# A fused GroupNorm and multi-scale linear attention kernel: TensorE's loop started at another point, its waits thinned, and two groups of small products mixed

## What is computed

```
xn  = group_norm(x, 32 groups)
qkv = einsum('nchw,oc->nohw', windows(xn, 4x4), qkv_w)
msq = concat([qkv, avg_pool5(qkv)], axis=1)          # full and pooled heads
q, k, v = relu(msq[..., :8]), relu(msq[..., 8:16]), msq[..., 16:]
v   = pad(v, one more column of ones)
kv  = einsum('ngld,nglm->ngdm', k, v)
out = einsum('ngld,ngdm->nglm', q, kv)
out = out[..., :-1] / (out[..., -1:] + 1e-15)
y   = einsum('nchw,oc->nohw', out, proj_w) * inv + offset
result = x + y
```

## Time and profile of the kernel before

| | |
|---|---|
| median of 3 runs | 928.52 us (928.47 to 930.1) |
| the profiled execution, its own time | 930.24 us |
| its span, first to last instruction | 928.3 us |
| around the span | 1.9 us |
| mean granted TensorE clock | 0.993 of full |
| TensorE matmul busy | 873.8 us, 94% |
| VectorE busy | 772.3 us, 83% |
| ScalarE busy | 609.5 us, 66% |
| GpSimd busy | 456.0 us, 49% |

### The profile page before, as it was taken

One profiled execution on the slowest core, in us unless ns is written; L12 is line 12 of the kernel. 1 busy time (PEld: TensorE's weight loads), 2 busy tenths in 40 slices (PEclk: granted clock), 3 DMA queues, 4 the chain that ended last, 5 costly groups with the idle time before them and its releaser, 6 DMA issues.

```text
span 928.3 us, 65376 instructions
## 1 busy us (share of the span) xinstructions
PE 873.8 (94%) x29282; PEld 733.4 (79%) x29282; DVE 772.3 (83%) x1625; ACT 609.5 (66%) x1542; POOL 456.0 (49%) x967
## 2 busy tenths in 40 slices
PE   0689999999999999999999999999999999999997
PEld 0578888888888888888888888888888888888885
DVE  7369989998878898998878998999887878787886
ACT  0457676767676767676766667676767676767673
POOL 1545454545454545555554545454545454545550
PEclk9999999999999999999999999999999999999998
DMA  9910000000000000000000000000000000000000
GB/s 378 431 50 17 26 17 26 17 26 17 25 19 25 26 17 26 17 26 17 26 17 26 18 26 17 26 17 27 17 26 17 25 25 18 26 17 26 18 26 27
DMA packets 15893, 38.77 MB, mean 42 GB/s; under 512 B 1888, under 2 KB 14688, under 8 KB 15456
## 3 DMA queue, kind: packets, MB, share of 16 engines
q1 hardware_dynamic: 15840, 38.26, 10.6%
HBM read 19.38 MB, written 18.87 MB: 41 GB/s over the span
## 4 chain that ended last, share of the span: by engine, by line
PE 93%; issue 3%; DVE 2%; POOL 1%; DMA 0%; ACT 0%; DVEq 0%; POOLq 0%
PE ps L611 23%; PE ps L582 19%; PE ps L538 14%; PE ps L549 9%; PE ps L556 9%; PE ps L633 7%; PE ps L627 6%; PE ps L635 4%; PE ps L558 4%; DVE stats L377 1%; DMA x_all<-x 0%; POOL hs L234 0%; DVE kvc_full L446 0%; POOL xp L234 0%; ACT o_sb L325 0%
## 5 line engine op out<-in xcount | busy, mean ns | idle before, releaser
L255 POOL TENSOR_TENSOR xn<-x_all,mean_t 128x384 f32<-128x384 f32 x96 | 79.4, 827 | 393.6 <-PE ps L558 375.1
L305 ACT ACTIVATE vm_pool<-ps,cst 128x256 f32<-128x256 f32 x576 | 225.5, 543 | 0.4 <-PE ps L549 0.4
L446 DVE TENSOR_TENSOR kvc_full<-ps,cst 128x864 f32<-128x864 f32 x192 | 193.7, 1050 | 17.8 <-PE ps L582 17.6
L446 DVE TENSOR_TENSOR kvc_pool<-ps,cst 128x864 f32<-128x864 f32 x192 | 193.2, 1048 | 0.0
L305 ACT ACTIVATE vm_full<-ps,cst 128x384 f32<-128x384 f32 x384 | 192.2, 598 | 0.9 <-PE ps L538 0.9
L312 ACT ACTIVATE q_full<-ps 128x384 f32<-128x384 f32 x96 | 47.2, 491 | 208.5 <-PE ps L556 208.5
L538 PE MATMUL ps<-wkv_sb,xn 128*128 128x128 f32 x1152 | 145.5, 276 | 23.5 <-POOL xn L256 23.5
L538 PEld LDWEIGHTS ps<-wkv_sb,xn 128*128 128x128 f32 x1152 | 144.1, 193 | 23.5 <-issue 23.5
L452 DVE SCALAR_TENSOR_TENSOR x_all<-ps,shift,x_all 128x384 f32<-128x384 f32 x96 | 59.3, 618 | 93.4 <-PE ps L633 93.2
L611 PEld LDWEIGHTS ps<-kvc_full,q_full 64*32 64x32 f32 x9216 | 99.5, 105 | 26.4 <-issue 26.3
L611 PE MATMUL ps<-kvc_pool,q_pool 64*32 64x72 f32 x9216 | 115.8, 230 | 2.1 <-issue 2.1
(11 more groups left out here) (66 smaller groups left out, 1242.2 us busy)
## 6 DMA issues: line engine op xcount, KB each, us to landing
out<-x_all SPq DMA_DIRECT2D x96, 192.0 KB, 1.9
x_all<-x SPq DMA_DIRECT2D x3, 4608.0 KB, 32.1
x_all<-x SPq DMA_DIRECT2D x6, 768.0 KB, 8.1
cst<-consts SPq DMA_DIRECT2D x1, 172.0 KB, 11.0
wkv_sb<-wkv SPq DMA_DIRECT2D x1, 128.0 KB, 10.8
o_sb<-proj SPq DMA_DIRECT2D x1, 128.0 KB, 10.4
wq_sb<-wq SPq DMA_DIRECT2D x1, 64.0 KB, 10.5
bn_sb<-bn SPq DMA_DIRECT2D x1, 2.0 KB, 10.3
```

Source lines behind the costliest of these rows:

```text
L255: link(pool.tensor_tensor(xr, src, mean, ALU.subtract), 1)
L305: last = act.activation(heads[:, :, e, :, 0:D], src, ACT.Copy, scale=col(mask + e))
L446: last = dve.tensor_tensor(kvc[:, g], src.to_broadcast(shape), own, ALU.mult)
```

## The change

TensorE's step is cut at another place of the same cycle. It now begins with transposes(s-1), and ends with Q(s+1) and the full K and V of s+2. The full kv products of strip s+1 no longer follow the pooled out products of strip s: the two are mixed in `out_pooled_and_kv`, two window groups of out products (32 instructions) and then one tile of kv products (16 instructions), three times. The waits of both stand ahead of the mixed block, among them the one for `y_done`. Waits that another wait implies are left out. `y_done` is no longer raised by the memset, and who waits for it waits for one less. Two steps at the start and two at the end now stand outside the loop, which has 46 rounds in place of 47. The other engines' streams are unchanged, but for the memset and SyncE's count.

```diff
-                    sp.wait_ge(y_done, t + (b * SPB + 2))
+                    sp.wait_ge(y_done, t + (b * SPB + 1))
...
-            dve.memset(dev[:], 0.0).then_inc(y_done, 1)
...
             def conv_kv_pooled(s, p):
                 pe.wait_ge(xp_ready, s + 1)
-                wait(pe, qm_f, s)
                 wait(pe, qm_p, s)
...
             def conv_q(s, p):
-                pe.wait_ge(km_p, s + 1)
                 pe.matmul(ps[:, Q_F, 0:SP], wq_sb[:], xn[:, p], start=True, stop=True).then_inc(q_f, 1)
-                pe.wait_ge(vm_p, s + 1)
                 pe.matmul(ps[:, Q_P, 0:SPP], wq_sb[:],
...
+            def kv_tile(pooled, t):
+                k, vm, bank, n = (k_pool, vm_pool, KVP, EP * KC) if pooled else (k_full, vm_full, KVF, EF * KC)
+                for r in range(G):
+                    rows = slice(H64 * r, H64 * (r + 1))
+                    for i in range(4):
+                        last = pe.matmul(ps[Q4 * i:Q4 * (i + 1), bank + r, t * n:(t + 1) * n],
+                                         k[rows, t, Q4 * i:Q4 * (i + 1)], vm[rows, t, :, i, :],
+                                         start=True, stop=True)
+                return last
...
+            def kv_products(s):
+                wait(pe, y_done, s - 1)
+                pe.wait_ge(vm_f, s + 1)
+                pe.nop(nofuse=True)
...
+            def kv_products_pooled(s):
+                pe.wait_ge(vm_p, s + 1)
+                wait(pe, num_f, s)
+                pe.nop(nofuse=True)
...
+            def out_products(s):
+                if is_last(s):
+                    pe.wait_ge(qm_p, s + 1)
+                pe.wait_ge(kvc_p, s + 1)
+                pe.nop(nofuse=True)
...
+            def out_pooled_and_kv(s):
+                pe.wait_ge(vm_f, s + 2)
+                wait(pe, y_done, s)
+                pe.nop(nofuse=True)
+                groups = [(t, e) for t in range(TP) for e in range(WP)]
+                for i in range(TF):
+                    for t, e in groups[QG * i:QG * (i + 1)]:
+                        last = out_tile(True, t, e)
+                    if i == TF - 1:
+                        last.then_inc(out_p, 1)
+                    last = kv_tile(False, i)
+                last.then_inc(kv_f, 1)
...
             def transposes(s):
-                pe.wait_ge(num_f, s + 1)
-                pe.wait_ge(num_p, s + 1)
                 if not is_last(s):
                     pe.wait_ge(kvc_f, s + 2)
                 else:
-                    pe.wait_ge(y_done, s + 1)
+                    pe.wait_ge(num_p, s + 1)
+                    pe.wait_ge(y_done, s)
...
             def step(s, p):
-                kv_products(s, False)
-                kv_products(s, True)
-                conv_q(s, p)
-                if not is_last(s):
-                    conv_kv(s + 1, 1 - p)
                 if not is_first(s):
                     transposes(s - 1)
                 if not is_last(s):
                     conv_kv_pooled(s + 1, 1 - p)
                 if not is_first(s):
                     project(s - 1)
-                out_products(s, False)
-                out_products(s, True)
+                out_products(s)
+                if is_last(s):
+                    out_products_pooled(s)
+                else:
+                    out_pooled_and_kv(s)
+                    kv_products_pooled(s + 1)
+                    conv_q(s + 1, 1 - p)
+                if not is_last(s) and not is_last(s + 1):
+                    conv_kv(s + 2, p)
...
+            kv_products(0)
+            kv_products_pooled(0)
+            conv_q(0, 0)
+            conv_kv(1, 1)
             step(0, 0)
-            with pe.Fori(1, NS - 1, 2) as s:
-                step(s, 1)
-                step(s + 1, 0)
-            step(NS - 1, (NS - 1) % 2)
+            step(1, 1)
+            with pe.Fori(2, NS - 2, 2) as s:
+                step(s, 0)
+                step(s + 1, 1)
+            step(NS - 2, 0)
+            step(NS - 1, 1)
```

More of the change, by code:

```diff
@@ L603, in out_products, with out_tile @@
+            def out_tile(pooled, t, e):
+                q, kvc, bank, wins = (q_pool, kvc_pool, OUTP, WP) if pooled else (q_full, kvc_full, OUTF, WF)
                 n = QG * KC
                 blocks = q[:].rearrange("p n e j -> p n (e j)")
[L605 to L613, removed]
@@ L614, in out_products @@
-                last.then_inc(done, 1)
+                for g in range(G):
+                    rows = slice(H64 * g, H64 * (g + 1))
+                    for c in range(4):
+                        r, w = c // QG, t * QG * wins + c % QG * wins + e
+                        last = pe.matmul(ps[Q4 * c:Q4 * (c + 1), bank + g, t * n:(t + 1) * n],
+                                         blocks[rows, 4 * t + c, Q4 * e:Q4 * (e + 1)], kvc[rows, r, w],
+                                         start=e == 0, stop=e == wins - 1)
@@ new lines, in out_tile @@
+                return last
+            def kv_products(s):
+                wait(pe, y_done, s - 1)
+                pe.wait_ge(vm_f, s + 1)
+                pe.nop(nofuse=True)
+                for t in range(TF):
+                    last = kv_tile(False, t)
+                last.then_inc(kv_f, 1)
[3 more added lines that the diff above has]
+                pe.nop(nofuse=True)
+                for t in range(TP):
+                    last = kv_tile(True, t)
+                last.then_inc(kv_p, 1)
@@ new lines, in out_products, with out_products_pooled @@
+            def out_products(s):
[3 more added lines that the diff above has]
+                pe.nop(nofuse=True)
+                for t in range(TF):
+                    for e in range(WF):
+                        last = out_tile(False, t, e)
+                last.then_inc(out_f, 1)
+            def out_products_pooled(s):
+                for t in range(TP):
+                    for e in range(WP):
+                        last = out_tile(True, t, e)
+                last.then_inc(out_p, 1)
```

## The result

The changed kernel takes **934.10 us** (median of 6 runs, 933.69 to 936.54), against 930.36 us for the kernel before (6 runs, 928.47 to 931.02): a ratio of 1.005, with a 95% interval of 1.0034 to 1.0066. It is slower, by 3.7 us, where 3 us of gain were forecast. The first three of the six runs of the kernel before are the ones behind the 928.52 us above. The profiled execution took 934.4 us, with a span of 932.6; it is set against the 930.24 and 928.3 of the one before.

What follows compares the result with a forecast made beforehand. TensorE with an exposed branch and a ring through ScalarE were taken to alternate as bound. Steady strips -5.1 us and cold code +2.1 gave -3.0: 925.5 us against the median, range 919.5 to 936.

Steps and rivals of the forecast that it cites:

- What bounds the kernel now: Steps alternate: 9.31 us, TensorE with the branch exposed, and 9.06 us, bound through ScalarE; shortening TensorE pays down to 9.06.
- The ring through ScalarE: Pooled kv, Q, ScalarE's relu_q and copies, then pooled kv again: 9.06 us a step, left as is by the change.
- the branch: The loop's compare-and-branch, 0.45 us in every second step; moved before the transposes, 0 left on the array, other bound 0.45.
- The dropped waits: Waits left out of TensorE's stream: 0.12 us gained between pooled out and full kv, nothing from the others, which are hidden.
- the ring through VectorE: Later out_p delays VectorE's pooled divide, then own_heads, statistics and residual: 9.08 us a step with bn_stats, 8.06 without.
- The mixed block: Mixed pooled out and full kv products: 1.72 us to the next pooled kv, nearly the plain sum of 1.74.
- D: Time from the mixed block's first matmul to the next pooled kv: 1.72 us taken, 1.52 to 2.28 possible.
- the slower rival: Changing between the two kinds of small matmul is not free; at D = 1.90 it gives 935.6 us; chance 0.25.
- The new wait and what is late next: The block waits for y_done, 0.2 us of new stall, hidden under 9.06; VectorE's pooled divide then waits for pooled out.
- the ring through the residual: From pooled kv through project and residual to the block's y_done wait: 7.21 + D = 8.93 us, hidden under 9.06.
- The assembling steps: Strips where VectorE assembles statistics: 10.14 and 9.88 us, 1.08 and 0.82 over 9.06, three times each, 5.7 us.
- Code run for the first time: Two more steps outside the loop or cold, one at either end: 1.05 us each, 2.1 us, bounds 0 and 4.

Runs made afterwards that it cites:

- w1_best_light: v2_best with one of the six masked copies of pooled V left out from strip 1 on (ScalarE lighter): 889.30 us, ratio 0.9563.
- u3_cut: The changed kernel, still mixed, with the loop cut after Q, so one step at each end stands outside as before: 930.88 us, ratio 1.0004.
- v1_swap: The changed kernel with the wait for num_f put before the wait for vm_p ahead of pooled kv: 931.92 us, ratio 1.002.
- b4_order: The kernel before with the wait for vm_p put ahead of the one for km_p in the pooled kv products: 931.84 us, ratio 1.0024.
- w2_mixed_light: v1_swap with one of the six masked copies of pooled V left out from strip 1 on: 930.57 us, ratio 1.0006.
- w3_plain_light: u1_plain with the two waits swapped and one of six masked copies of pooled V left out from strip 1 on: 925.14 us, ratio 0.9944.
- u1_plain: The changed kernel with its block not mixed, all pooled out products before full kv, waits still ahead of the block: 932.34 us, ratio 1.0017.
- u2_late: The changed kernel not mixed, with the wait for y_done put back between pooled out and full kv: 929.28 us, ratio 0.9984.
- b1_peel_start: The kernel before with two more TensorE steps ahead of the loop: 935.26 us, ratio 1.0068.
- v2_best: The changed kernel not mixed, y_done's wait between pooled out and full kv, loop cut after Q, num_f's wait before vm_p's: 919.68 us, ratio 0.9895.
- u4_both: The changed kernel not mixed, y_done's wait between pooled out and full kv, loop cut after Q, waits not swapped: 924.76 us, ratio 0.9936.
- b2_peel_end: The kernel before with two more TensorE steps behind the loop: 936.86 us, ratio 1.0081.

## Why the prediction was wrong

- **What bounds the kernel now: right.** The ring through ScalarE binds the 9.06 us steps and the branch makes the 9.31. w1_best_light moves the step by exactly what ScalarE loses.
- **The branch: right.** No cost of it shows at either cut, in the changed kernel and in u3_cut. The pattern of two is gone, and in w1_best_light, with the cut of u3_cut, it doesn't come back at 8.70.
- **The dropped waits: the step that failed.** "The others are hidden: nothing", said the prediction. One that was dropped ahead of pooled out does give TensorE 0.11 us (full out to pooled out, above), off the binding ring. And a dropped wait changes which condition stands first in the instruction that is left, and this one lies on the binding ring: +0.044 us a step, 92 x 0.04 = 3.7 us. Shown from both sides by v1_swap and b4_order. In the steps with bn_stats the ring through VectorE gives 9.10 as well, by v1_swap and w2_mixed_light, where the forecast had 9.08; so the swap alone brings back 2.2 us and not 3.7.
- **The mixed block: right in the main.** D was put at 1.72 and is 1.74; the 1.89 of the changed kernel's trace contains a wait for ScalarE. That mixing would cost (the slower rival, 0.25) gave the sign that came, but it is not the mechanism: w2_mixed_light and w3_plain_light differ by 0.01 us.
- **The new wait and what is late next: right, a little small.** Plain steps hide both; the ring through the residual measures 8.98 to 9.00 where 8.93 was forecast. The assembling steps, with the three behind each pair of them, cost 6.5 us where 5.7 were forecast. Of these, 3.4 are the wait ahead of the block (u1_plain keeps them, u2_late doesn't), and 3.1 are out_p's lateness by mixing.
- **Code run for the first time: the second step that failed, a term mis-sized.** 2.1 us were forecast for the two steps, within 0 to 4. The changed kernel's trace has 0.3 + 4.6 + 1.0 = 5.9, and the isolated cost is 5.1 at the start and 7.0 at the end for two steps, that is 6 for one at either end. The 1.05 a step that I had from the two gaps of the earlier trace rows was far too small: the three gaps shown of b1_peel_start alone are 4.3 us.
- **The sum.** Forecast -3.0. The order of waits +3.7, the cold code +3.8, the assembling steps +0.8, and -0.7 for the 36 strips whose own 0.02 is inside the 9.10: together +7.6, which makes +4.6, against 4.2 measured in the profiled executions (934.4 less 930.24). The range ended at 936 and held the time; the sign was wrong. That it held the time is owed to the room left for the slower rival, whose mechanism isn't what happened. Each of the two failed steps is about large enough to use up the 3.0 us, and taking away only one of them does not bring the gain back: with the order put right the kernel is still slower than the one before (v1_swap, 1.002), and with no more steps outside the loop than before it is level with it (u3_cut, 1.0004). No run has both put right with the block mixed. v2_best shows what the new step is good for when the loop is cut behind Q, some 10 us, and the other variants where the changed kernel gives it back: the order of two waits, two more cold steps, and in twelve strips the early wait and the mixing.

## What to carry to other kernels

Before pricing a wait at nothing, ask whether it shares an instruction with the wait that binds: put the condition that comes last in the last place, and look again after dropping any. A group of instructions that looks longer after a change may only be stretched by who it waits for at its end; take that waiter away before calling it the cost. And choose a loop's cut so that it hides the branch and also leaves as few steps as possible outside: here both were to be had at once, and v2_best, cut behind Q, without the mixing and with the wait for `y_done` late, is 1.05% faster than the kernel before.

## What the runs showed of the hardware

- A wait instruction of TensorE's sequencer with two conditions starts 37 to 38 ns after the first of them, if that one is late, and takes 51 ns more; if the second is late, it ends 44 ns after it. The late-first order costs 44 ns each time (u4_both against v2_best, and b4_order against the kernel before).
- Small matmuls on tiles of 64 by 32 with 72 and with 144 columns take the same time mixed and in two blocks: 2.68 and 2.67 us from the first to the following Q (w2_mixed_light, w3_plain_light).
- Small products on different tiles do not start strictly in program order: in w3_plain_light four full kv products start after the first pooled kv product, by up to some 50 ns.
- A step of TensorE's code, some 610 instructions, costs 2.5 us more the first time it runs near the start and 3.5 near the end (half of +5.1 in b1_peel_start and of +7.0 in b2_peel_end, whose intervals overlap), and 5 packets more on the instruction queue go with two such steps.
